# Two attention layers with output projection and layer norm, eight cores: how softmax sums are made and staged, how filler is dealt out, and what the output tiles wait for

## The chip, the cores and the metric

One Trainium2 chip; the program runs on all 8 cores, each on one of the 8 sequences of the batch, without exchange between cores. The metric is the device time in microseconds (us) of the slowest core, median of several runs. Engines are called PE (TensorE, matmul), DVE (VectorE), ACT (ScalarE), POOL (GpSimd) and SP (SyncE, here only a DMA queue).

## The reference

```python
def attn(x, Wqkv, bqkv, Wo, bo):            # 16 query heads of 128, ONE k and v head
    qkv = x @ Wqkv.T + bqkv                 # x: (8, 2048, 2048)
    s = q @ k.T / sqrt(128), causal;  p = softmax(s);  ctx = p @ v
    return ctx @ Wo.T + bo
def ffn(x, Wa, Wp, w_std, w_rec):           # 16 heads with q, k and v of their own
    fused = x @ (Wa * col_scale)            # 120 "std" + 8 "low" columns a head for q and k
    # low columns of q and k change places where w_rec > 0.1
    s = Qf @ Kf.T / sqrt(128), causal;  return concat(softmax(s) @ V) @ Wp
x = layernorm(x + attn(x));  x = layernorm(x + ffn(x))
```

A core does 2048 rows by 2048 columns in bf16 matmuls with f32 accumulation.

## The kernel before

**Program.** A Python builder (`Prog`) writes down each engine's instructions in order. Every operation gives a token (semaphore, count) and may wait for tokens of others. Within an engine the order is exactly the order in which the builder was called, so that where a line stands in the builder is where it stands in the queue. Loads that cast f32 to bf16 go through POOL's queue; all other transfers go through SP's queue.

**Stages.** (1) x transposed (`xT`, in `bufB`) and the weights of k, v and the first q are loaded and projected. (2) `at1`: attention of 16 heads with the q projections of later heads as filler for PE. (3) `outproj`: context (`bufA`) times `wo` (in `bufB`), plus residual and bias, layer norm; rows are stored and a transposed copy is put into `bufA`. (4) `at2`: attention of 16 heads with q, k and v projections as filler. (5) `outproj` again with `wp`.

**One head.** The transposed scores are made in 20 steps (`STEPS`): four windows w of 512 queries; in window w, 2w "full" steps (two key blocks of 128 by 512 queries), then step "a" (512 + 384 columns) and step "b" (256 + 128 columns) on the diagonal, whose corners POOL masks. `WIN_END` is (1, 5, 11, 19). A step g counts on over all heads. `scores(g)` fills one of two banks `s_ps`, ACT's exp writes `pt` (four buffers), `values(g)` adds v times pt into `c_ps`, and at the end of a window ACT copies `c_ps` to one of the `cf` buffers. The loop `run` issues in step g: scores(g+1); hooks; `todo` (below); filler from a stream of generators until a target count is reached (`feed`, one unit is one matmul of 512 columns, 0.5 for one of 256); values(g-1); `lsum`.

**Softmax sums.** DVE adds the pt tiles of a window to `acc` (1024 columns), then folds its halves to 512 (`sums`). `split_hi` (ACT) and `split_lo` (DVE) make bf16 hi and lo of it; `lsum` lets PE add over the partitions with a band of ones, each window into 32 rows of `l_ps` of its own. `recip` (DVE) inverts `l_ps` in `r4`; SP stores one row of each window to DRAM (`rr_d`) and `bcast` loads it back into all partitions (`rb`); `norm` (DVE) multiplies `cf` by `rb` into the context. `plan` says at which step of this or the next head each is issued. at1 has two rb and six cf buffers, at2 one rb and five cf. Parameter `lag` (1 in at1, 0 in at2, 1 in at2's last head) delays split and lsum by that many steps and puts the sums of the next tile behind lo in DVE's queue. Window 0 is summed in `acc[:, 512:1024]`; a new window may be added only when lo of the old one has read acc. Windows 0 to 2 of the last head go the same way into buffers of their own (`rb_last`), window 3 in `tail` by ones-matmuls on hi and lo to all partitions.

**Shift.** For each head `stats` (a small matmul and a DVE maximum) and `shift` (a small matmul and a DVE maximum, `mbias`) estimate the exponent's offset. Both use the bank of `pj0`/`pj1` that the next filler group will use, whose first matmul then waits for them. `insert(n, ...)` places them n units further down the stream. A filler group (16 matmuls, or 32 of half the size) is 16 units.

**Around the last head.** After the last projection the streams give idle units (42 in at1, 46 in at2), then `early_tiles`: 14 of the 16 head terms of two output tiles. Big weight loads (2048 KB, four for each projection) are issued on POOL at the steps given in `at_step`, the last two after the loop. `outproj` then does parts of six tiles (heads 0 to 14), `tail`, z loads (SP; POOL adds the bias), and the rest. A tile is 16 matmuls into one of eight banks; DVE adds it to z and frees the bank. z buffers lie over q, pt, acc and k of the attention.

## Time and profile before

| | |
|---|---|
| median of 3 runs | 2178.45 us (2171.26 to 2179.46) |
| the profiled execution's own time | 2177.09 us |
| its span, slowest core (6) | 2175.2 us |
| spans of the eight cores | 2150.7 to 2175.2 us |
| PE busy | 1988.3 us, 91% |
| DVE busy | 1178.8 us, 54% |
| ACT busy | 1011.5 us, 46% |
| POOL busy | 263.1 us, 12% |

The profile is one execution. Busy time of PE counts matmuls, whose ends are modelled; weight loads run beside them. The clock is the one granted to PE as a part of full speed. "Idle before" is what an engine waited before a group, with the engine that ended it. In DVE and PE rows the name left of the arrow is written, those on the right are read; L298 is the projections' matmul, L412 scores, L424 exp, L574 values, L812 output tiles, L691 early output tiles, L540 norm, L513 reciprocal, L80 any DMA.

### The profile page before, as it was taken

The page shows a single profiled execution, that of the slowest core. Times are in us where ns is not written, and L with a number is a line of the kernel's source. Part 1 is how long each engine was busy: PE and PEld are TensorE (multiplying, and loading weights), DVE is VectorE, ACT ScalarE, POOL GpSimd, SP SyncE. Part 2 cuts the span into 40 slices and gives each one's busy share as a digit, 9 for nine tenths or more (in the row PEclk, how much of TensorE's full clock was granted, in tenths as well). Part 3 has the DMA queues.
Part 4 walks back from the last instruction along what each step waited for, and adds up shares of the span by engine and source line. Part 5 has one row for each costly group of instructions (what it writes and reads, how often), then busy time and mean ns, then how long its engine had stood idle before and what let it go on. Part 6 is the DMA issues. An engine that isn't in the chain of part 4 may idle for free.

```text
span 2175.2 us, 30749 instructions; the slowest of 8 cores (2150.7 to 2175.2 us)
## 1 busy us (share of the span) xinstructions
PE 1988.3 (91%) x10400; PEld 1007.4 (46%) x10400; DVE 1178.8 (54%) x1931; ACT 1011.5 (46%) x1403; POOL 263.1 (12%) x354
## 2 busy tenths in 40 slices
PE   5999898989877999999999999999999999769997
PEld 2444343434333444464655646464554646324443
DVE  0167878788876365314554545555554555543433
ACT  0266776777763343315454453535454453532221
POOL 2011111111111344100010100100010000110000
PEclk9788999999998999999999999999999999889999
DMA  9521212121136798612122212212122110375751
GB/s 145 89 39 30 50 40 52 38 54 35 38 60 112 173 278 236 166 31 37 40 50 49 49 31 45 44 30 59 40 49 49 45 35 16 59 119 139 223 206 78
DMA packets 94981, 171.68 MB, mean 79 GB/s; under 512 B 38126, under 2 KB 62830, under 8 KB 85484
## 3 DMA queue, kind: packets, MB, share of 16 engines
q0 software_dynamic: 33216, 59.77, 17.6%
q1 hardware_dynamic: 61612, 109.94, 17.4%
q8 instruction: 87, 1.43, 0.3%
q14 instruction: 66, 0.54, 0.1%
HBM read 187.26 MB, written 33.81 MB: 102 GB/s over the span
## 4 chain that ended last, share of the span: by engine, by line
PE 80%; DMA 7%; issue 4%; DVE 4%; ACT 3%; POOL 2%; DVEq 0%; SPq 0%; ACTq 0%; POOLq 0%; another core or an unknown queue 0%
PE pj L298 29%; PE pj L1016 10%; PE c_ps L574 10%; PE s_ps L412 9%; PE s_ps L812 9%; PE pj L812 4%; PE c_ps L812 2%; PE l_ps L812 2%; DMA bufB<-xT 2%; ACT pt L424 1%; DMA rb<-rr_res 1%; PE l_ps L505 1%; PE l_ps L506 1%; DMA rl<-rr_res 1%; DMA bufB<-wo 1%
## 5 line engine op out<-in xcount | busy, mean ns | idle before, releaser
L424 ACT ACTIVATE pt<-s_ps,mbias 128x1024 bf16<-128x1024 f32 (+2 forms) x640 | 631.0, 988 | 577.5 <-PE s_ps L412 493.1
L298 PE MATMUL pj<-bufA,ws 128*128 128x512 bf16 x2048 | 485.2, 381 | 17.8 <-DVE mbias L394 16.1
L574 PE MATMUL c_ps<-pt,v 128*128 128x512 bf16 (+3 forms) x1280 | 350.3, 356 | 43.4 <-ACT cf L584 34.7
L298 PEld LDWEIGHTS pj<-bufA,ws 128*128 128x128 bf16 x2048 | 199.0, 98 | 250.5 <-issue 26.8
L468 DVE TENSOR_TENSOR acc<-acc,pt 128x1024 f32<-128x1024 f32 x192 | 235.5, 1226 | 129.2 <-ACT pt L424 120.4
L298 PE MATMUL pj<-bufB,ws 128*128 128x512 bf16 x1024 | 288.8, 396 | 1.2 <-DVE mhat L381 0.7
L432 POOL TENSOR_SCALAR_AFFINE_SELECT pt<-pt 128x256 bf16<-128x256 bf16 x256 | 139.5, 546 | 988.4 <-ACT pt L424 986.5
L1016 PE MATMUL pj<-wv,bufA 128*128 128x256 bf16 x2048 | 240.0, 273 | 14.2 <-DVE mbias L394 13.5
L1016 PEld LDWEIGHTS pj<-wv,bufA 128*128 128x128 bf16 x2048 | 199.2, 98 | 53.4 <-issue 16.6
L574 PEld LDWEIGHTS c_ps<-pt,v 128*128 128x128 bf16 x1280 | 122.9, 99 | 200.2 <-issue 99.8
L837 ACT ACTIVATE sqs<-z 128x512 f32<-128x512 f32 x128 | 80.6, 629 | 247.6 <-DVE z L832 235.2
L495 DVE TENSOR_TENSOR lo<-acc,hi 128x512 bf16<-128x512 f32 x128 | 88.4, 690 | 184.9 <-ACT hi L490 180.9
L412 PE MATMUL s_ps<-q,kT 128*128 128x512 bf16 (+3 forms) x640 | 176.3, 359 | 2.2 <-ACT pt L424 1.8
L412 PE MATMUL s_ps<-q,k 128*128 128x512 bf16 (+3 forms) x640 | 172.8, 352 | 0.1
L298 PEld LDWEIGHTS pj<-bufB,ws 128*128 128x128 bf16 x1024 | 101.0, 101 | 113.8 <-issue 40.6
L462 DVE TENSOR_TENSOR acc<-pt,pt 128x1024 f32<-128x1024 bf16 x96 | 116.7, 1216 | 32.6 <-ACT pt L424 27.3
L812 PE MATMUL s_ps<-bufB,bufA 128*128 128x512 bf16 x512 | 116.1, 387 | 7.5 <-DVE bufA L540 5.8
L812 PE MATMUL s_ps<-bufA,bufB 128*128 128x512 bf16 x512 | 116.8, 389 | 0.0
L471 DVE TENSOR_TENSOR acc<-acc,pt 128x512 f32<-128x512 f32 x96 | 67.7, 705 | 90.0 <-POOL pt L432 89.9
L513 DVE RECIPROCAL r<-l_ps 128x512 f32<-128x512 f32 (+1 forms) x32 | 107.2, 3351 | 0.1
L584 ACT COPY cf<-c_ps 128x512 f32<-128x512 f32 x127 | 74.2, 584 | 56.5 <-PE c_ps L574 56.3
L412 PEld LDWEIGHTS s_ps<-q,k 128*128 128x128 bf16 x640 | 62.7, 99 | 71.3 <-issue 5.9
(110 smaller groups left out, 1770.7 us busy)
## 6 DMA issues: line engine op xcount, KB each, us to landing
rb<-rr_res SPq DMA_DIRECT2D x120, 256.0 KB, 3.5
ws<-wqk POOLq DMA_DIRECT2D x32, 512.0 KB, 5.2
z<-x SPq DMA_DIRECT2D x16, 1024.0 KB, 6.5
x_res<-z SPq DMA_DIRECT2D x16, 1024.0 KB, 6.4
z<-x_res SPq DMA_DIRECT2D x16, 1024.0 KB, 6.5
out<-z SPq DMA_DIRECT2D x16, 1024.0 KB, 7.2
ws<-wq POOLq DMA_DIRECT2D x16, 512.0 KB, 6.1
bufB<-wo POOLq DMA_DIRECT2D x4, 2048.0 KB, 27.4
```

The costliest lines, as they stand in the source:

```text
L298: tok = P.pe(lambda t, c=c, b=b: t.matmul(pj[b][:, :], lhs(c), rhs(c), start=(c == 0), stop=(c == NCH - 1)), waits=wt, inc=(c == NCH - 1))
L412: last = t.matmul(sp[:, o:o + n], k[:, c * 128:(c + 1) * 128], q[:, w * 512 + q0:w * 512 + q0 + n], start=True, stop=True)
L424: self.exp_tok[g] = P.ac(lambda s: s.activation(pt[:, 0:n], sp[:, 0:n], AF.Exp, bias=mbias[h % 2][:, :]), waits=[self.s_tok[g], self.mb_ok ...
L432: ok = P.gp(lambda g_: g_.affine_select(out=blk, in_=blk, pattern=[[0, 2], [1, 128]], compare_op=ALU.is_ge, fill=0.0, base=0, channel_mult ...
L462: t = P.ve(lambda v: v.tensor_add(acc[:, :], p0[:, :], pt[:, :]), waits=[ok, self.p_ok[g - 1], self.hl_src_read])
L468: t = P.ve(lambda v: v.tensor_add(acc[:, :], acc[:, :], pt[:, :]), waits=[ok, self.acc_ok])
L495: self.lo_ok = P.ve(lambda v: v.tensor_sub(self.lo[:, :], src, self.hi[:, :]), waits=[self.hi_ok, self.fold_ok, self.hl_free])
L513: self.r_tok[h] = P.ve(lambda v: v.reciprocal(self.r4[0:n, :], l_ps[0:n, :]), waits=[self.l_tok[h], self.ro_tok.get(h - 1)])
L574: last = t.matmul(c_ps[:, q0:q0 + n], self.vbuf(h)[:, c * 128:(c + 1) * 128], pt[:, o:o + n], start=(beg and n_ == 0), stop=(end and n_ == 1))
L812: last = t.matmul(banks[b], ctx[:, h * S + j * 128:h * S + (j + 1) * 128], wbuf[:, (ew * H + h) * 512:(ew * H + h + 1) * 512], start=(h == ...
L837: state["sq"] = P.ac(lambda s: s.activation(sqs[:, :], zc, AF.Square, accum_out=cq[:, ew:ew + 1]), waits=[t, state["sq"]])
L1016: tok = P.pe(lambda t, tt=tt, c=c, s0=s0: t.matmul(pj[b][:, tt * 256:(tt + 1) * 256], bufA[:, s0:s0 + 128], wv2[:, c * 256:(c + 1) * 256], ...
```

## The change

- xT lies in `bufB` by windows: [w][c][512] instead of [c][w 512]. So the quarter of window 0 is free for the first quarter of `wo` as soon as the last q group of window 0 is done, and it is loaded there. wp's first quarter is loaded at the last k projection.
- `fold_out` (at1): the fold of acc goes to a buffer of its own (`f1`), window 0 is summed there; hi and lo are double; a third rb.
- Steps of split, lsum, recip, norm and bcast are given by lists; in at1 split is at (3, 7, 13, 21) instead of (2, 6, 12, 20), lsum at (8, 9, 15, 22) instead of (5, 8, 14, 21), recip at 3 instead of 2, bcast at (6, 7, 8, 12) instead of (4, 5, 9, 11), norm at (10, 12, 14, 16) instead of (9, 11, 14, 16). In at1 the next sums stand between hi and lo.
- at1's filler is uneven: weight 6.0 at steps 1, 3, 7 and 13, else 2.5, of 64 a head (before 3.2 each); its lead falls from 36 to 30 units over the heads.
- Last head of both: no sums on DVE. `last_sums` multiplies each pt by a 128x128 of ones into pj0 or pj1, straight to all partitions; a reciprocal of the bank, then the norm, at each window's end. `tail` is gone.
- One whole early tile (16 matmuls, in `l_ps`, the first bank in the new order of banks) instead of two of 14; idle units 60 and 56.
- Output tiles wait for the norms of their own window of 512 rows in heads 14 and 15; z loads wait for the end of the last head's values (at1's fourth for its last norm).
- at2: `shift` at 22 units instead of 13.5. Last two quarters of wo and wp are loaded at step 13 of the last head.

```diff
-    hi1 = row("hi1", 36864, 512, BF16)
-    lo1 = row("lo1", 37888, 512, BF16)
+    hi1 = [row("hi1_0", 36864, 512, BF16), row("hi1_1", 24576, 512, BF16)]
+    lo1 = [row("lo1_0", 37888, 512, BF16), row("lo1_1", 25600, 512, BF16)]
+    f1 = [row(f"f1_{i}", 26624 + 2048 * i, 512, F32) for i in range(2)]
...
+    rb1.append(row("rb1_2", 30720, 512, F32))
...
+            t = P.dma("gpsimd", f"xt{w}_{i}", xT3[:, w, i * n:(i + 1) * n, :],
...
+        def sources(self, w):
+            if self.fold_out:
+                return (self.fold[0][:, :], 0) if w == 0 else (self.fold[1][:, :], 1)
+            return (self.acc[:, 512:1024], 0) if w == 0 else (self.acc[:, 0:512], 1)
...
+            if h == H - 1:
+                return
...
-                if w > 0:
-                    t = P.ve(lambda v: v.tensor_add(acc[:, 0:512], acc[:, 0:512],
-                                                    acc[:, 512:1024]), waits=[t])
-                self.fold_ok = t
+                self.fold_ok[w] = P.ve(lambda v: v.tensor_add(src, acc[:, 0:512],
+                                                              acc[:, 512:1024]),
+                                       waits=[t] + ([self.src_read[1]] if self.fold_out else []))
...
+            rb = self.rb[n] if h < H - 1 else self.fold[w % 2]
...
+        def last_sums(self, g):
+            h, i = g // NST, g % NST
+            w, kind, chunk = STEPS[i]
+            pt = self.pt[g % 4]
+            pcs = pieces(w, kind, chunk)
+            beg, end = i == WIN_BEG[w], i == WIN_END[w]
+            b = (w + 1) % 2
             ones = strip[:, 96:97].broadcast_to([128, 128])
             def mm(t):
-                t.matmul(l_ps[:, :], ones, self.hi[:, :], start=True, stop=False)
-                return t.matmul(l_ps[:, :], ones, self.lo[:, :], start=False, stop=True)
-            t = P.pe(mm, waits=[self.hi_ok, self.lo_ok, self.r_tok[h]])
-            for i in range(NW - 1):
-                self.norm(h, i)
-            self.rb_ok[(h, w)] = P.ve(lambda v: v.reciprocal(self.r4[:, :], l_ps[:, :]),
-                                      waits=[t, self.ro_tok[h]])
-            self.norm(h, w)
+                last = None
+                for n_, (c, q0, o, n) in enumerate(pcs):
+                    last = t.matmul(pj[b][:, q0:q0 + n], ones, pt[:, o:o + n],
+                                    start=(beg and n_ == 0), stop=(end and n_ == 1))
+                return last
+            t = P.pe(mm, waits=[self.p_ok[g], tok_strip] + ([pj_free[b]] if beg else []))
+            if end:
+                rb = self.fold[w % 2]
+                self.rb_ok[(h, w)] = P.ve(
+                    lambda v: v.reciprocal(rb[:, :], pj[b][:, :]),
+                    waits=[t, self.norm_tok[(h, w - 2)] if w > 1 else None] + self.src_read)
+                pj_free[b] = self.rb_ok[(h, w)]
...
+            if h == H - 1:
+                self.last_sums(g)
             t = P.pe(mm, waits=[self.p_ok[g], self.v_ok[(h, chunk)], self.v_ok[(h, chunk + 1)]] +
...
+                if h == H - 1:
+                    self.norm(h, w)
...
+            for h in range(H - 1):
+                g0, g1 = h * NST, (h + 1) * NST
                 for w in range(NW):
-                    if last and w == NW - 1:
-                        continue
-                    put(g0 + WIN_END[w] + lag, "split", h, w)
-                    put(g0 + self.l_at[w] + (lag if w < NW - 1 else 0), "lsum", h, w)
-                if last:
-                    put(g0 + 14 + lag, "recip", h)
-                    for w in range(NW - 1):
-                        put(g0 + 14 + lag, "bcast", h, w)
-                else:
-                    g1 = g0 + NST
-                    norm_at = self.norm_at if h < H - 2 else self.norm_at_last
-                    bc_at = self.bc_at if h < H - 2 else self.bc_at_last
-                    put(g1 + self.r_at, "recip", h)
-                    for w in range(NW):
-                        put(g1 + norm_at[w], "norm", h, w)
-                    for w in range(NW):
-                        put(g1 + bc_at[w], "bcast", h, w)
+                    put(g0 + self.split_at[w], "split", h, w)
+                    put(g0 + self.l_at[w], "lsum", h, w)
+                    put(g1 + self.norm_at[w], "norm", h, w)
+                    put(g1 + self.bc_at[w], "bcast", h, w)
+                put(g1 + self.r_at, "recip", h)
...
-                lag = self.lag if h < H - 1 or i == 0 else self.lag_last
-                if lag == 0 and g + 1 < n:
+                if not self.fold_out and g + 1 < n:
                     self.sums(g + 1)
                 for what, hh, w in todo:
                     if what == "split":
                         self.split_hi(w)
+                if self.fold_out and g + 1 < n:
+                    self.sums(g + 1)
                 for what, hh, w in todo:
                     if what == "split":
                         self.split_lo(w)
-                if lag == 1 and g + 1 < n:
-                    self.sums(g + 1)
...
+    at1 = Att("a1", 0, lambda h: kT, lambda h: q1[h % 2], lambda h: v1, bufA, pt1, acc1, f1,
+              True, hi1, lo1, cf1, rb1, r41, (3, 7, 13, 21), (8, 9, 15, 22), 3,
+              (6, 7, 8, 12), (10, 12, 14, 16))
...
+    def early_tile(att, ctx, wbuf, w_tok):
+        for h in range(H):
+            def mm(t, h=h):
+                return t.matmul(l_ps[:, :], ctx[:, h * S:h * S + 128],
+                                wbuf[:, h * 512:(h + 1) * 512], start=(h == 0),
+                                stop=(h == H - 1))
+            att.tile = P.pe(mm, waits=[w_tok[0], att.norm_tok[(h, 0)], att.r_tok[H - 2]],
+                            inc=(h == H - 1))
+            yield 1.0
...
+            if w == 0 and h == H - 1:
+                wo_tok.append(load_big(bufB, wo_d, 0, [tok]))
...
+    fill = [6.0 if i in (1, 3, 7, 13) else 2.5 for i in range(NST)]
+    def lead1(h):
+        return 36.0 - 6.0 * min(h, H - 1) / (H - 1)
     def target1(h, i):
-        return 64.0 * h + LEAD1 + 64.0 * (i + 1) / NST
+        a, b = 64.0 * h + lead1(h), 64.0 * (h + 1) + lead1(h + 1)
+        return a + (b - a) * sum(fill[:i + 1]) / sum(fill)
...
-    at1.at_step[(H - 2) * NST + 11] = lambda tok: wo_tok.append(
-        load_big(bufB, wo_d, 0, [xt_end[0], tok]))
-    at1.at_step[(H - 1) * NST + 10] = lambda tok: wo_tok.append(
+    at1.at_step[(H - 2) * NST + 13] = lambda tok: wo_tok.append(
         load_big(bufB, wo_d, 1, [xt_end[0], tok]))
+    at1.at_step[(H - 1) * NST + 13] = lambda tok: wo_tok.extend(
+        load_big(bufB, wo_d, i, [xt_end[0], tok]) for i in (2, 3))
     at1.run(target1)
-    for i in (2, 3):
-        wo_tok.append(load_big(bufB, wo_d, i, [xt_end[0]]))
...
-            b = turn[0] % 8
+            b = (7, 1, 2, 3, 4, 5, 6, 0)[turn[0] % 8]
...
+        def normed(w):
+            return [att.norm_tok[(h, w)] for h in (H - 2, H - 1)]
...
-        last = [att.norm_tok[(H - 2, NW - 1)]]
-        fin = {}
-        heads(2, 2, 0, range(H - 1), last + [w_tok[0], bank_free[2]], False)
-        att.tail()
-        for jj in first_z:
-            load_z(jj, zfree + [att.norm_tok[(H - 1, NW - 2)]])
-            add_bias(jj)
-        bank_free[7] = att.rb_ok[(H - 1, NW - 1)]
-        heads(3, 3, 0, range(H - 1), [bank_free[3]], False)
-        for j in (0, 1):
-            heads(j, j, 0, [H - 2], [], False)
-        for j in (0, 1):
-            heads(4 + j, j, 1, range(H - 1), [w_tok[1], bank_free[4 + j]], False)
-        for n in range(6):
-            fin[n] = heads(n, n % 4, n // 4, [H - 1], [att.norm_tok[(H - 1, NW - 1)]], True)
-        for n in range(4):
-            evict(n, n, 0, fin[n])
-        for n in range(6):
-            next_bank()
-        evict(4, 0, 1, fin[4])
-        evict(5, 1, 1, fin[5])
-        for ew in (1, 2, 3):
-            for j in range(2 if ew == 1 else 0, 4):
+        for j in first_z:
+            load_z(j, zfree[j])
+            add_bias(j)
+        for ew in range(4):
+            for j in range(4):
                 b = next_bank()
-                t = heads(b, j, ew, range(H), [w_tok[ew], bank_free[b]], True)
+                t = att.tile
+                if ew + j > 0:
+                    t = heads(b, j, ew, range(H),
+                              [w_tok[ew], bank_free[b]] + normed(0), True)
...
-                t = heads(b, j, ew, range(H), [bank_free[b]], True)
+                t = heads(b, j, ew, range(H),
+                          [bank_free[b]] + normed(j // 4), True)
...
+                            [[at1.pv_done[H - 1]]] * 3 + [[at1.norm_tok[(H - 1, NW - 1)]]], tok_bo, finish1,
...
+              acc2, f2, False, hi2, lo2, cf2, rb2, r42, (1, 5, 11, 19), (4, 6, 12, 20), 1,
+              (3, 5, 7, 9), (5, 7, 9, 11))
...
+                    wp_tok.append(load_big(bufA, wp_d, 0, [tok]))
...
-            at2.insert(13.5, lambda h=h: at2.shift(h))
+            at2.insert(22.0, lambda h=h: at2.shift(h))
...
-        for u in idle(46):
+        for u in idle(56):
             yield u
-        for u in early_tiles(at2, bufB, bufA, wp_tok):
+        for u in early_tile(at2, bufB, bufA, wp_tok):
...
+    at2.at_step[(H - 1) * NST + 7] = lambda tok: wp_tok.append(
         load_big(bufA, wp_d, 1, [x2_end[0], tok]))
+    at2.at_step[(H - 1) * NST + 13] = lambda tok: wp_tok.extend(
+        load_big(bufA, wp_d, i, [x2_end[0], tok]) for i in (2, 3))
```

## Rows read from the trace of the kernel before

**Rows 1.** The cores: span and mean granted clock, slowest core.

```profile
core 6: 2175.2 us, clock 0.964
```

**Rows 2.** Windows of core 6: length, busy us (instructions) of each engine, clock, DMA share, GB/s.

```profile
core 6: us, PE busy (x) PEld busy (x) DVE busy (x) ACT busy (x) POOL busy (x), PEclk, DMA share, GB/s
95.00:205.00 110.00, 106.71 (x434) 45.50 (x433) 75.30 (x101) 73.55 (x92) 14.02 (x25) 0.81 0.18 34
205.00:624.40 419.40, 372.91 (x1810) 170.25 (x1809) 337.88 (x456) 298.99 (x374) 60.99 (x103) 1.00 0.18 41
624.40:733.00 108.60, 77.57 (x317) 31.48 (x316) 58.45 (x77) 37.82 (x51) 32.10 (x23) 0.86 0.77 138
...
980.00:1870.00 890.00, 861.38 (x5016) 487.96 (x5015) 472.47 (x736) 425.19 (x529) 74.61 (x149) 0.99 0.19 41
1875.50:1962.50 87.00, 55.39 (x209) 21.77 (x208) 44.09 (x53) 28.27 (x35) 10.33 (x14) 0.79 0.73 114
1962.50:2163.00 200.50, 200.50 (x929) 90.76 (x927) 76.65 (x231) 49.86 (x142) 0.00 (x0) 1.00 0.50 165
```

**Rows 3.** Waits of PE, 160 to 590: us in total, times, longest.

```profile
PE c_ps L574 <- ACT cf L584: 24.8, 43, 1.1
PE l_ps L505 <- DVE r L513: 18.1, 12, 1.9
```

**Rows 4.** DVE's groups by form, 160 to 590: busy, mean ns; idle before, releaser.

```profile
L513 DVE RECIPROCAL r<-l_ps 128x512 f32<-128x512 f32 x12 | 40.2, 3352 | 0.0
L495 DVE TENSOR_TENSOR lo<-acc,hi 128x512 bf16<-128x512 f32 x48 | 33.1, 690 | 51.9 <-ACT hi L490 47.8 <-ACT cf L584 4.0
```

**Rows 5.** Waits of PE, 980 to 1870.

```profile
PE pj L298 <- DVE mbias L394: 16.1, 7, 2.3
PE pj L1016 <- DVE mbias L394: 12.6, 7, 1.8
```

**Rows 6.** Waits of PE, 0 to 95.

```profile
PE pj L298 <- DMA bufB<-xT: 26.1, 7, 13.7
```

**Rows 7.** PE in order of time, 590 to 740: start, us, what; idle before, releaser.

```profile
650.38 0.59 PE L691 MATMUL pj<-bufB,bufA 128*128 128x512 bf16 x1 [7.51 <-DMA bufB<-wo]
...
687.27 6.19 PE L812 MATMUL s_ps<-bufB,bufA 128*128 128x512 bf16 x15 [5.80 <-DVE bufA L540]
...
708.10 1.01 PE L812 MATMUL pj<-bufB,bufA 128*128 128x512 bf16 x2 [4.06 <-DVE bufA L540]
```

**Rows 8.** POOL in order of time, 600 to 735.

```profile
680.95 2.32 POOL L80 DMA_DIRECT2D bufB<-wo  x2
...
714.05 17.92 POOL L825 TENSOR_TENSOR z<-z,bo_sb 128x2048 f32<-128x2048 f32 x4 [29.16 <-DMA z<-x]
```

**Rows 9.** The chain that ended last, in order of time: start, us, what.

```profile
1880.33 17.35 DMA bufA<-wp
1909.18 2.97 DMA rb<-rr_res
1913.01 6.49 DMA rb<-rr_res
1920.35 8.46 DMA rb<-rr_res
...
1936.79 5.19 DMA rr_res<-r
```

**Rows 10.** PE in order of time, 1850 to 1980.

```profile
1885.66 0.58 PE L505 MATMUL l_ps<-hi,strip 128*128 128x512 bf16 x1 [3.25 <-DVE lo L495]
...
1897.82 1.44 PE L691 MATMUL pj<-bufA,bufB 128*128 128x512 bf16 x3 [7.63 <-DMA bufA<-wp]
...
1932.52 0.91 PE L574 MATMUL c_ps<-pt,v 128*128 128x512 bf16 x2 [4.60 <-POOL pt L432]
...
1959.96 1.01 PE L812 MATMUL pj<-bufA,bufB 128*128 128x512 bf16 x2 [5.29 <-DVE bufB L540]
```

**Rows 11.** DVE in order of time, 1860 to 1980.

```profile
1886.85 3.36 DVE L513 RECIPROCAL r<-l_ps 128x512 f32<-128x512 f32 x1
```

More of the change, by code:

```diff
@@ L220, in build_program @@
     acc2 = row("acc2", 36864, 1024, F32)
-    hi2 = row("hi2", 40960, 512, BF16)
-    lo2 = row("lo2", 41984, 512, BF16)
+    hi2 = [row("hi2", 40960, 512, BF16)]
+    lo2 = [row("lo2", 41984, 512, BF16)]
+    f2 = [row(f"f2_{i}", 38912 - 2048 * i, 512, F32) for i in range(2)]
     cf2 = [row(f"cf2_{i}", 43008 + 2048 * i, 512, F32) for i in range(5)]
@@ L684, in idle @@
             yield 1.0
-    def early_tiles(att, ctx, wbuf, w_tok):
-        for j in (0, 1):
-            for h in range(H - 2):
-                wt = [w_tok[0], att.norm_tok[(h, NW - 1)], pj_free[j]]
-                P.pe(lambda t, j=j, h=h: t.matmul(
-                    banks[j], ctx[:, h * S + j * 128:h * S + (j + 1) * 128],
-                    wbuf[:, h * 512:(h + 1) * 512], start=(h == 0), stop=False),
-                    waits=wt, inc=False)
-                yield 1.0
+    def early_tile(att, ctx, wbuf, w_tok):
[7 more added lines that the diff above has]
+            yield 1.0
     def q1_group(h, w):
```

158 lines of the change are left out of this document (63 added, 95 removed).

## The prediction, made before the changed kernel ran

> **What bounds the kernel now.** I read the cores first: the slowest is core 6, at 2175.2 us [rows 1]; the execution's own time is 2177.09 us, so 1.9 us lie around the span. The windows of core 6 [rows 2] cut it into stages. TensorE (PE) does nearly all of the path: the second output projection runs at 100% busy and clock 1.00, 929 matmuls in 200.5 us, 0.2158 us each. So a gain can come only where PE is idle or at a lower clock. That is: 46.5 us in the first attention at full clock (205 to 624.4), 28.6 us in the second (980 to 1870), 31.0 us at the first change-over (clock 0.86), 31.6 us at the second (clock 0.79). From 95 to 205 the clock is 0.81 and PE idles only 3.3 us.
>
> What PE waits for in the first attention [rows 3]: in 430 us, 43 times for ScalarE's (ACT's) copy cf out of c_ps (24.8 us), 12 times for VectorE's (DVE's) reciprocal (18.1 us). The rows by form of DVE [rows 4] show one reciprocal of 3.35 us a head, 12 in 430 us: a head takes 35.8 us. They also show DVE idle 47.8 us before the 48 subtractions lo, waiting for ACT's hi: 4.0 us a head.
>
> In the second attention [rows 5] every wait of PE is for mbias, the shift, 14 times, 28.7 us.
>
> **Change, start of the program.** xT lies in blocks of w instead of c. PE waits 26.1 us for xT [rows 6], 13.7 of it for the first piece. The same bytes come in the same ten transfers, so at best the later 12 us shrink (half of it if larger pieces help), at worst nothing: 0 to -6, I take -0.5.
>
> **First attention, per head.** No operation is added or taken; order, buffers and waits change. (a) hi, lo move one step later: cf is now ahead of hi in ACT's queue, where hi waits for the fold. (b) lo stands behind the next sums, so DVE works where it waited 4.0 us. (c) `lsum` of window 0, which must wait for the reciprocal of the head before, is issued at step 8 and the reciprocal at 3: PE's wait for it (18.1/12 = 1.5 us a head) has five steps of cover, against three. (d) Filler: 6 units at steps 1, 3, 7, 13, just where `values` waits for cf, instead of 3.2. That puts 2.8 x 0.2158 = 0.6 us more work ahead of a wait whose mean is 24.8/43 = 0.58 us. The other steps get 0.7 units (0.15 us) less. So both PE waits should go. The floor is now double. PE: 372.91/419.4 x 35.8 = 31.8 us a head. DVE: 337.88/419.4 x 35.8 = 28.8 busy; of its idle 6.9, the 4.0 for hi can go and the rest are hand-overs: 31.8 as well. Two engines with equal floors, coupled by four pt buffers, and cf(2) that waits (on ACT) for the norm of the head before, which stands behind a late DVE: they don't both reach it. I take 32.6 us, so 3.2 x 11.7 heads = -37. Bounds: -46 (all idle), -12 (DVE late, 1 us a head). In the stretch at clock 0.81 PE is nearly full: 0 to -3.3, I take -2.
>
> **First change-over.** Before: projections end at 624.4, the projection's matmuls at 916, 291.6 us. After: head 14 has 11 steps left without filler. PE needs some 8 us for them, but DVE still sums them. Before, PE stood at the early tiles at 642.9 (650.38 less 7.51 [rows 7]), 18.5 us later and two steps further; I take 16. Head 15: scores, values and now ones-matmuls, each 17408 columns = 34 x 0.2158 = 7.3 us, together 22.0; the early tile 16 x 0.2158 = 3.5; the last band sums 0.4: 26, of which 1.5 overlap the tail before. DVE loses all sums of that head and gets four reciprocals (3.35 each) for two. Stalls 3 us: the last lo, and the norm of head 14, behind two reciprocals in a row (15's first, then 14's), which the tile's 15th matmul wants at step 13. Then 63 tiles x 3.453 = 217.5, for which only the norms of window 0 are needed, long done. Sum 16 + 24.5 + 3 + 217.5 = 261: -30. What goes by name: 7.51 (wo), 5.80 and 4.06 (the norms) [rows 7]. What may come late next: z is loaded from the end of head 15 and POOL adds the bias in 17.92/4 = 4.5 us each [rows 8]; as before about 10 us until z is there, then four adds, 14 to 28 us. PE needs its first bank again after seven tiles, 24 us, and that bank waits only for z0. Covered by 10 us. The two big loads in front of the last two masks on POOL cost 2.32 us of issue [rows 8], under five steps of about 1.3 us: nothing; without that cover 2.3. Bounds: -37 and -20.
>
> **Second attention.** `shift` goes from 13.5 to 22 units behind its head's last projection. A group is 16 units; before, the shift used the bank that the group starting 2.5 units later needs, and PE waited 28.7/14 = 2.05 us for DVE. Now the bank's next group begins ten units (2.2 us) and about one attention step later: 2.05 + 0.54 = 2.6 us of latency under some 3 us. mbias itself is needed 14 units later at the earliest. So -29; at least -5, if DVE's queue is late by more than one sum of 1.2 us.
>
> **Second change-over.** Before: from 1875.5 to 2163.1, 287.6 us. wp starts with the last projection, 5 us earlier, and lands at about 1875.7 + 17.35 + 0.8 = 1894 [rows 9]; PE, which stood at step 3 at 1890.2 (1897.82 less 7.63 [rows 10]), comes to the tile three steps and 4 us later, also about 1894: the 7.63 goes. Of the other idle the 3.25 for lo stays, the 4.60 for a mask (behind DVE's late sums) and the 5.29 for the norms go [rows 10]. Of head 15's 26 us some 6 are done at 1894; with 4 us of stalls (ACT's copy of window 1 waits for head 14's first norm) PE would be through at about 1918. But at2 has one rb buffer, so head 14's four broadcasts go one by one, each after the norm before. And the second tile now goes to bank 1, which is pj1, free only after the reciprocal of window 2, which stands on DVE behind the last of those norms. Chain: reciprocal 1886.85 + 3.36 [rows 11]; store 5.19 to 1895.4; first broadcast 3 to 6.5, norm and hand-over 0.9 (1913.01 less 1909.18 + 2.97), 1900.5; three more beside the wp loads at 6.49 to 8.46 [rows 9] plus 0.9, 25.2; 1926; reciprocal 3.35, 1929.5; 2 us for a PE that restarts at half clock (1.2 GHz, as in the 15 matmuls in 6.19 us [rows 7]). 1931.5 + 217.5 = 2149: -14. Ends: all broadcasts as quick as the free one (2.97 [rows 9]) makes PE the limit, -27; 12 us each gives +3.
>
> The DMA share of this chain is where a rule bears. The rows show a broadcast at 2.97 us alone and 8.46 beside the loads [rows 9]. The Trainium skill (DMA: Bandwidth & Descriptors, section Queues, rings and completion order) says each DMA engine takes turns between queue rows: two more loads in POOL's queue would then not slow SP's broadcasts further, and the sum stands. If they shared by transfer, four at once would make 4 x 2.97 = 12 us, two broadcasts later by 4 each, 8 us worse. Only before and after together can tell.
>
> **Sum.** -0.5 - 2 - 37 - 30 - 29 - 14 = -112.5. On the execution's own 2177.09: 2064.6; the median of the runs, 2178.45, lies 1.4 above: 2066.
>
> **Rivals.** (1) DVE becomes the bound of the first attention: its floor equals PE's [rows 2, 4]; for it, a queue with a 3.35 us reciprocal in one lump; against it, four pt buffers. A head of 34.8 us: 25 lost, 2091. (2) The shift's wait moves instead of going, at the other bank, behind DVE's copies of v: 24 lost, 2090. (3) "Tiles wait for their own block" isn't so where banks bind: the chain through bank 1 is longer (12 us broadcasts), or the same one binds in at1 too: 15 lost, 2081. Against it in at1: three rb buffers, and window 2's reciprocal stands before the last two norms. (4) Slower: PE denser on all cores draws the clock of 0.81 over the attention. Its price: PE's 861 us in the second attention alone become 861/0.81, +202; it decides once some 480 us more of full PE run at 0.81 (112/0.235), 2066 + 202 = 2268 for that stage. For it: 95 to 205 [rows 2]. Against it: 200.5 us at 100% busy and clock 1.00. The Trainium skill (TensorE: Matmul & The Clock Gate, Part 1) has a limiter that holds a die at 13/16 once three of its cores run dense matmuls; the row of the output projection speaks against it here.
>
> **Chances.** Forecast 0.65; (1) 0.13, (2) 0.08, (3) 0.10, (4) 0.04. Range: all good ends together 2029, all bad 2144; neither is likely, 2046 (PE near its floor in both) to 2104 (rivals 1 to 3, or two of them in part) leaves out 0.2. Its own range for the forecast is 2046 to 2085. Half a per cent, about what a measurement of this kernel can tell from no change, is 11 us; only the last rival and a heap of misses reach it: faster 0.94, same 0.02, slower 0.04.
>
> **What will show it.** Right: one reciprocal each 32 to 33 us in the first attention, no waits for cf or r at `values` and `lsum`, DVE over 90% there; no PE wait for mbias in the second; no gap over 2 us between head 15 and the tiles in at1; in at2 a PE gap before the second tile that DVE's reciprocal ends, at about 1929 less what went before. Wrong: ACT waiting for DVE's sums or norms in each head, a granted clock under 1.00 for long, or tiles waiting for z.

## The result, and the profile after

The changed kernel takes 2054.37 us (median of four executions, three of which lie between 2052.94 and 2055.14), 0.9443 of before's time (95% interval 0.9418 to 0.9468): 5.6% faster. I had forecast 2066, with a range of 2046 to 2104. Of both kernels some executions are longer, with four cores at a lower clock (here one of 2308.19 us, at 0.85 to 0.87), and all ratios, and the times given further down, leave these out.

The profiled execution took 2052.94 us. Its cores, with mean granted clock:

```profile
core 0: 2041.3 us, clock 0.991
...
core 7: 2051.1 us, clock 0.989
```

Before, the slowest core had a clock of 0.964 [rows 1]; now none is under 0.988. The windows of core 7, at the landmarks used in the prediction (last projection at 567.5 and 1767, last matmul of the two output projections at 835.3 and 2038.9):

```profile
core 7: us, PE busy (x) PEld busy (x) DVE busy (x) ACT busy (x) POOL busy (x), PEclk, DMA share, GB/s
95.00:205.00 110.00, 105.26 (x521) 49.41 (x519) 90.28 (x121) 85.82 (x109) 17.49 (x30) 1.00 0.16 35
205.00:567.50 362.50, 342.12 (x1694) 162.02 (x1693) 318.27 (x428) 276.99 (x350) 63.21 (x97) 1.00 0.23 52
567.50:617.50 50.00, 41.62 (x194) 18.28 (x192) 37.55 (x38) 34.38 (x40) 10.98 (x16) 0.93 0.57 99
617.50:835.30 217.80, 217.76 (x1011) 98.56 (x1008) 98.56 (x237) 77.45 (x158) 73.95 (x20) 1.00 0.88 214
980.00:1767.00 787.00, 783.00 (x4656) 452.28 (x4655) 436.26 (x679) 382.56 (x476) 67.20 (x135) 1.00 0.20 43
1767.00:1819.10 52.10, 33.86 (x160) 15.30 (x158) 23.71 (x20) 25.90 (x31) 9.34 (x14) 0.84 0.89 147
1819.10:2038.90 219.80, 219.76 (x1008) 99.01 (x1008) 81.71 (x234) 49.83 (x142) 0.00 (x0) 0.99 0.52 157
```

From these landmarks, slowest core against slowest core, and core 0 against core 0 (in us). The last projection of the first attention ends at 623.7 in before, not at 624.4 where the prediction cut its windows:

| up to / between | before, core 6 | after, core 7 | difference | core 0 | predicted |
|---|---|---|---|---|---|
| start to last projection of attention 1 | 623.7 | 567.5 | -56.2 | -43.9 | -39.5 |
| to the end of output projection 1 | 292.4 | 267.8 | -24.6 | -20.0 | -30 |
| to the last projection of attention 2 | 959.4 | 931.7 | -27.7 | -32.5 | -29 |
| to the end of output projection 2 | 287.6 | 271.9 | -15.7 | -13.1 | -14 |
| sum | | | -124.2 | -109.5 | -112.5 |

Core 0's first attention ran at clock 1.00 in both kernels, while cores 6 and 7 of before had 0.81 from 95 to 205 [rows 2]. It is one of six such cores, and the six don't agree closely: their sums go from -107.9 to -126.0, with a mean of -115.0. The means of the four stages are -44.6, -23.9, -30.4 and -16.1.

The waits of PE (us in total, times, longest) from 160 to 560 of after:

```profile
PE l_ps L523 <- DVE lo L512: 19.4, 25, 1.2
PE pj L394 <- ACT q L702: 2.4, 4, 0.7
PE pj L301 <- DVE mhat L384: 0.8, 1, 0.8
```

The waits for ACT's cf and for DVE's reciprocal, 24.8 and 18.1 us in 430 us [rows 3], are gone. In their place stands a wait at the same matmul (L505 is now L523) for lo. DVE over the same stretch waits for the masks, and no longer for hi: the second fence, its groups by form, has no idle ahead of the 49 subtractions lo, against 51.9 us [rows 4]. DVE is busy for 350 of these 400 us, 87.5%:

```profile
DVE acc L487 <- POOL pt L435: 27.9, 33, 1.8
```

```profile
L512 DVE TENSOR_TENSOR lo<-f,hi 128x512 bf16<-128x512 f32 x49 | 36.0, 735 | 0.0
```

From 980 to 1767, where PE lost 28.7 us to mbias [rows 5], it waits only for this:

```profile
PE pj L394 <- DVE v L1016: 4.0, 7, 0.6
```

The first change-over, PE in order of time. The tiles start without a gap; the gaps for wo and for the norms [rows 7] are gone:

```profile
597.30 0.38 PE L690 MATMUL l_ps<-bufB,bufA 128*128 128x512 bf16 x1 [2.35 <-DVE r L530]
...
617.37 0.33 PE L588 MATMUL c_ps<-pt,v 128*128 128x256 bf16 x2
617.53 3.62 PE L817 MATMUL pj<-bufB,bufA 128*128 128x512 bf16 x16
```

The second, PE and then DVE. Of the waits for wp and for a mask [rows 10] only 0.23 us are left, but the second tile stands 11.44 us:

```profile
1776.99 0.59 PE L523 MATMUL l_ps<-hi,strip 128*128 128x512 bf16 x1 [3.96 <-ACT cf L601]
...
1807.21 0.33 PE L567 MATMUL pj<-pt,strip 128*128 128x256 bf16 x2 [0.23 <-POOL pt L435]
1819.14 5.67 PE L817 MATMUL pj<-bufA,bufB 128*128 128x512 bf16 x16 [11.44 <-DVE f L574]
```

```profile
1776.15 0.69 DVE L512 TENSOR_TENSOR lo<-acc,hi 128x512 bf16<-128x512 f32 x1 [1.78 <-ACT hi L506]
1778.17 3.36 DVE L530 RECIPROCAL r<-l_ps 128x512 f32<-128x512 f32 x1 [1.33 <-PE l_ps L524]
...
1788.14 0.69 DVE L545 TENSOR_TENSOR bufB<-cf,rb 128x512 bf16<-128x512 f32 x1 [2.23 <-DMA rb<-rr_res]
...
1796.81 0.69 DVE L545 TENSOR_TENSOR bufB<-cf,rb 128x512 bf16<-128x512 f32 x1 [3.84 <-DMA rb<-rr_res]
1806.10 0.69 DVE L545 TENSOR_TENSOR bufB<-cf,rb 128x512 bf16<-128x512 f32 x1 [8.60 <-DMA rb<-rr_res]
1815.03 0.69 DVE L545 TENSOR_TENSOR bufB<-cf,rb 128x512 bf16<-128x512 f32 x1 [8.23 <-DMA rb<-rr_res]
1815.64 3.35 DVE L574 RECIPROCAL f<-pj 128x512 f32<-128x512 f32 x1
```

This is the chain: the reciprocal of head 14, four norms (L545) each waiting for its broadcast, and only then the reciprocal of window 2 (L574) that frees bank 1 for the second tile.

### The profile page after: what moved, and what is told of

Its sections match the earlier page's. It is cut to its first block, busy times and chain, and to the rows that moved or that the text cites. A ratio compares the mean times of both kernels' runs of the same rounds, so it can differ in the third digit from the quotient of the medians.

```text
span 2051.1 us, 30678 instructions; the slowest of 8 cores (2037.6 to 2051.1 us)
## 1 busy us (share of the span) xinstructions
PE 1946.3 (95%) x10464; PEld 1006.8 (49%) x10464; DVE 1146.5 (56%) x1871; ACT 1001.6 (49%) x1395; POOL 261.5 (13%) x354
## 4 chain that ended last, share of the span: by engine, by line
PE 73%; DVE 10%; issue 5%; ACT 5%; DMA 4%; POOL 2%; DVEq 0%; another core or an unknown queue 0%; ACTq 0%; POOLq 0%; SPq 0%
PE pj L301 24%; PE s_ps L817 11%; PE pj L1007 10%; PE s_ps L415 7%; PE c_ps L588 7%; PE pj L817 5%; ACT pt L427 4%; PE c_ps L817 3%; DVE r L530 3%; PE l_ps L817 2%; DMA bufB<-xT 2%; DMA rb<-rr_res 2%; POOL pt L435 1%; DVE acc L489 1%; PE l_ps L523 1%
## 5 line engine op out<-in xcount | busy, mean ns | idle before, releaser
L588 PE MATMUL c_ps<-pt,v 128*128 128x512 bf16 (+3 forms) x1280 | 341.9, 349 | 4.0 <-ACT cf L601 3.7
L484 DVE TENSOR_TENSOR acc<-acc,pt 128x1024 f32<-128x1024 f32 x180 | 220.5, 1225 | 126.9 <-ACT pt L427 123.8
L301 PE MATMUL pj<-bufB,ws 128*128 128x512 bf16 x1024 | 272.6, 379 | 2.0 <-DVE mhat L384 1.5
L415 PE MATMUL s_ps<-q,kT 128*128 128x512 bf16 (+3 forms) x640 | 170.6, 349 | 2.1 <-ACT pt L427 2.1
L478 DVE TENSOR_TENSOR acc<-pt,pt 128x1024 f32<-128x1024 bf16 x90 | 109.3, 1215 | 36.6 <-ACT pt L427 33.7
L817 PE MATMUL s_ps<-bufA,bufB 128*128 128x512 bf16 x512 | 111.8, 379 | 0.0
L512 DVE TENSOR_TENSOR lo<-acc,hi 128x512 bf16<-128x512 f32 x60 | 42.9, 715 | 111.3 <-ACT hi L506 108.4
L840 DVE SCALAR_TENSOR_TENSOR z<-s_ps,z 128x512 f32<-128x512 f32 x64 | 43.5, 689 | 105.0 <-PE s_ps L817 94.7
L530 DVE RECIPROCAL r<-l_ps 128x512 f32<-128x512 f32 x30 | 100.4, 3348 | 1.3 <-PE l_ps L524 1.3
```

Of the source, the lines that this page charges most:

```text
L301: tok = P.pe(lambda t, c=c, b=b: t.matmul(pj[b][:, :], lhs(c), rhs(c), start=(c == 0), stop=(c == NCH - 1)), waits=wt, inc=(c == NCH - 1))
L415: last = t.matmul(sp[:, o:o + n], k[:, c * 128:(c + 1) * 128], q[:, w * 512 + q0:w * 512 + q0 + n], start=True, stop=True)
L478: t = P.ve(lambda v: v.tensor_add(acc[:, :], p0[:, :], pt[:, :]), waits=[ok, self.p_ok[g - 1], self.fold_ok[w - 1] if w > 1 else self.fold ...
L484: t = P.ve(lambda v: v.tensor_add(acc[:, :], acc[:, :], pt[:, :]), waits=[ok, self.acc_ok])
L530: self.r_tok[h] = P.ve(lambda v: v.reciprocal(self.r4[:, :], l_ps[:, :]), waits=[self.l_tok[h], self.ro_tok.get(h - 1)])
L588: last = t.matmul(c_ps[:, q0:q0 + n], self.vbuf(h)[:, c * 128:(c + 1) * 128], pt[:, o:o + n], start=(beg and n_ == 0), stop=(end and n_ == 1))
```

## Experiments

Ratios are to before. The changed kernel run again (e0_after) shows how far two runs of one kernel differ: 0.9463 (0.9447 to 0.9478), median 2056.97; so 0.002 can be noise. In its profile the gap ahead of the second tile was 15.14 us.

> The kernel after, unchanged, as the reference for the three beside it. A head of its first attention takes 33.0 us; all its windows should be as in its first profile, within 3 us in total.

**The shift alone**, in the kernel before.

```diff
-            at2.insert(13.5, lambda h=h: at2.shift(h))
+            at2.insert(22.0, lambda h=h: at2.shift(h))
```

> The kernel before with one edit: the second attention's shift stands 22 units behind the last projection of its head instead of 13.5. My theory (the wait for mbias disappears under the next filler group) expects the 28.7 us of waits in the second attention to go and nothing else to change: 29 us less than before, ratio 0.987. The rival (the wait moves to the other bank, behind the copies of v) expects 5 us less at most, ratio 0.998.

0.9846 (0.9831 to 0.9862), 2138.83 us against 2171.85: -33. From 980 to 1830 all waits for mbias went; one of another kind is left:

```profile
PE pj L391 <- DVE v L1025: 4.0, 7, 0.6
```

The span from output projection 1 to the last projection is 931.0 us here and 931.7 in after. So this edit makes the whole gain of that stage, and the wait did not move to the other bank. It gives 4 us more than the waits held. The trace of before shows where they lie. Its core 0 waits for mbias no longer than core 6 (28.5 us), but in five places the clock granted to PE falls while or just after it waits (0.83 to 0.92 over the 10 us from 1004, 1124, 1244, 1494 and 1614), and its stage takes 964.4 us; core 6 has three such places and 959.4. In after no stretch of 10 us from 980 to 1767 is under 1.00, nor in this run to 1832. So in some places a wait of 2.3 us cost its own length and some 3 us at half clock after it (core 0, 1130 to 1132: clock 0.50).

**The old schedule of attention 1 in the changed kernel**: buffers and both change-overs of after; the order of sums and lo, steps and filler of before (the lead of the filler stays that of after).

```diff
-    fill = [6.0 if i in (1, 3, 7, 13) else 2.5 for i in range(NST)]
+    fill = [3.2 for i in range(NST)]
...
-(3, 7, 13, 21), (8, 9, 15, 22), 3, (6, 7, 8, 12), (10, 12, 14, 16)
+(2, 6, 12, 20), (5, 8, 14, 21), 2, (4, 5, 9, 11), (9, 11, 14, 16)
```

> The kernel after with the schedule of the kernel before in the first attention: even filler, split at 2, 6, 12, 20, lsum at 5, 8, 14, 21, reciprocal at 2, broadcasts and norms at the old steps, lo ahead of the next sums. What stays of the change there is room alone: folds in buffers of their own, hi and lo double, a third rb. Theory A (the order made the gain, each part of it sharing it with the others): a head goes back to 35 us or more, 28 to 38 us slower than after. Rival B (room made the gain: the next window's sums need not wait for lo): a head stays under 34 us, less than 14 us slower. Lo first alone cost 3 to 4 us and even filler alone 9, so their sum, 13, is what B would expect at most.

2088.94 and 2090.55 us; two executions, too few for a ratio: +32 to +36. The reciprocals give the head's length: 14 of them from 134.5 to 593.1 are 35.3 us a head. PE's waits from 160 to 560 are those of before again:

```profile
PE c_ps L588 <- ACT cf L601: 24.0, 46, 0.9
PE l_ps L523 <- DVE r L530: 15.3, 11, 1.5
```

With 36.0 a head in before (below) and 33.0 in after, the order is worth 2.3 us a head and the rest, the doubled and separate buffers among it, some 0.7.

**Only the splits back to the old steps**, a step earlier.

```diff
-(3, 7, 13, 21), (8, 9, 15, 22), 3,
+(2, 6, 12, 20), (8, 9, 15, 22), 3,
```

> The kernel after with only the splits back at steps 2, 6, 12, 20 in the first attention, so that ACT's hi stands ahead of the copy cf again. If hi ahead of cf, waiting for the fold, was what kept PE waiting at the window ends, a head grows by 1 to 2 us, 14 to 28 us slower than after. If the filler of 6 units covers it as well, or VectorE is the bound anyway: within 5 us of after.

0.9597 (0.9583 to 0.9611), median 2087.59: +29 to +33. Reciprocals 133.8 to 590.5 (14): 35.1 a head. From 160 to 560, PE's wait and then ACT's:

```profile
PE c_ps L588 <- ACT cf L601: 33.8, 23, 2.6
```

```profile
ACT hi L506 <- DVE f L499: 35.9, 23, 2.6
```

The same count, the same longest wait: ACT stands at hi for the fold, cf stands behind it, and PE waits for cf. Step (a) taken back alone takes back nearly all that the old schedule does (2.1 of 2.3 us a head).

It does so by other waits than those of before. Here PE waits 23 times, 1.5 us on average; in before 43 times, 0.58 [rows 3], and with the whole old schedule 46 times, 0.52. There ACT hardly waits for the fold: 8.3 us in the 430 of before, 0.5 at most, and 5.3 in the 400 of the old schedule. What the copy cf waits for in before is mostly hi itself, which stands ahead of it in ACT's queue, as ACT's rows show for the wait of 0.51 that PE has at 596.74:

```profile
595.50 0.61 ACT L490 CAST hi<-acc 128x512 bf16<-128x512 f32 x1
596.00 0.59 ACT L584 COPY cf<-c_ps 128x512 f32<-128x512 f32 x1
```

In between lie the place of lo, the filler and the later steps, which this run keeps from after; which of them makes the long waits isn't shown. So this run shows that the new order needs (a); whether (a) alone would have brought the gain to the kernel before, no run shows.

**lo ahead of the next sums again**: the two blocks of `run` exchanged for attention 1.

```diff
-                if self.fold_out and g + 1 < n:
-                    self.sums(g + 1)
                 for what, hh, w in todo:
                     if what == "split":
                         self.split_lo(w)
+                if self.fold_out and g + 1 < n:
+                    self.sums(g + 1)
```

> The kernel after with lo put ahead of the next tile's sums again in VectorE's queue, in the first attention only. Theory (VectorE is the second floor of a head there, 33.0 us measured, and the new order saved it 4.0 us a head of waiting for hi): the head grows by 1 to 3 us, 14 to 40 us slower than after, the waits of lo for hi come back. Rival (the gain of the first attention came from the filler and from lsum's later step alone): under 5 us slower.

0.9461 (0.9444 to 0.9478): no difference that can be told, where I expected 14 to 40 us. The head stays 33.0 (129.2 to 591.1, 15 reciprocals). DVE stands 26.9 us ahead of lo again (the trace puts 7.9 to hi and 19.0 to PE's scores), and PE waits 9.2 for lo instead of 19.4, but also for mhat and cf:

```profile
PE l_ps L523 <- DVE lo L512: 9.2, 13, 1.0
PE pj L301 <- DVE mhat L384: 4.4, 6, 1.3
PE c_ps L588 <- ACT cf L601: 4.1, 6, 1.2
```

Step (b) only exchanges one wait for others.

**Even filler**, `fill = [3.2 for i in range(NST)]`.

> The kernel after with even filler in the first attention, 3.2 units at every step instead of 6.0 at four and 2.5 at sixteen. Theory: the waits of PE for the copy cf come back, four of about 0.6 us a head, but part of them only takes the place of waits for VectorE, which is as full as PE: 10 to 30 us slower than after. Rival (uneven filler does nothing, since hi no longer stands ahead of cf): within 5 us.

0.9486 (0.9471 to 0.9501), all four executions between 2059.88 and 2060.88: +5 to +9 us. Reciprocals 131.0 to 600.6 (15): 33.5 a head, half a microsecond more. But the waits for cf don't come back:

```profile
PE l_ps L523 <- DVE lo L512: 23.7, 24, 2.0
PE c_ps L588 <- ACT cf L601: 1.5, 1, 1.5
```

So step (d) is worth about what I gave it (0.6 us), not for the reason that I gave: the filler's 6 units don't cover cf, since with (a) nothing waits for cf anyway.

**DVE made lighter**: in attention 1 every plain "full" sum adds only the first 512 of its 1024 columns, so the row sums are incomplete.

```diff
             elif kind == "full":
-                t = P.ve(lambda v: v.tensor_add(acc[:, :], acc[:, :], pt[:, :]),
+                c = 512 if self.fold_out else 1024
+                t = P.ve(lambda v: v.tensor_add(acc[:, 0:c], acc[:, 0:c], pt[:, 0:c]),
```

> The kernel after, with half of the columns left out of the plain additions of full tiles (the 1024-column additions after a window's first) in the first attention: VectorE has some 3 us less to do in a head, PE exactly the same. If VectorE's floor binds a head (31.8 us by my estimate, against 31.8 for PE), the head falls from 33.0 to 31.5 or less, 20 us or more faster than after. If PE's own work and its small waits make the 33.0: under 8 us faster. In between: both floors bind in turn, which is my theory: 8 to 20 us faster.

0.9392 (0.9373 to 0.9410): -11 to -15 us; reciprocals 134.0 to 579.8 (15), 31.8 a head. PE's first wait from 160 to 560, and the window (PE, PEld, DVE, ACT, POOL):

```profile
PE l_ps L524 <- DVE lo L513: 9.0, 21, 1.1
```

```profile
160.00:560.00 400.00, 389.03 (x1926) 184.18 (x1924) 323.11 (x484) 315.99 (x400) 56.33 (x110) 1.00 0.24 53
```

A head falls by 1.2 us and stops at PE's floor of 31.8 [rows 2], with PE at 97%. DVE thus costs attention 1 the 1.2 us between the floor and 33.0. That PE pays it at `lsum` suggests a cheaper way to give it back:

**`lsum` and reciprocal later.**

```diff
-(3, 7, 13, 21), (8, 9, 15, 22), 3,
+(3, 7, 13, 21), (8, 10, 15, 23), 4,
```

> The kernel after with lsum at steps 8, 10, 15, 23 instead of 8, 9, 15, 22 and the reciprocal at 4 instead of 3, in the first attention: the two lsum of a head that PE waits for (27 waits for lo, 20.4 us in 450) come one step later. If PE's small waits add straight to the time: 15 to 20 us faster than after. If VectorE, which is busy nearly without a break, is the bound of a head, the time stays within 5 us. The lighter VectorE of the run before gave 15 us, so I expect something between: 5 to 12 us faster.

0.9425 (0.9400 to 0.9449); against after -4 to -8 us, at the edge of what can be told by its time. The trace is plainer: reciprocals 134.6 to 582.4 (15), 32.0 a head, and the wait for lo is gone:

```profile
PE pj L301 <- DVE mhat L384: 7.2, 5, 2.3
PE c_ps L588 <- ACT cf L601: 3.2, 4, 1.5
...
PE l_ps L523 <- DVE lo L512: 0.7, 1, 0.7
```

No work was taken from DVE. So what bound the head at 33.0 was not DVE's amount of work but that PE asked for lo too early.

**Bank 1 last in the turn.** The tiles of both output projections take their banks in another order.

```diff
-            b = (7, 1, 2, 3, 4, 5, 6, 0)[turn[0] % 8]
+            b = (7, 2, 3, 4, 5, 6, 1, 0)[turn[0] % 8]
```

> The kernel after with the output tiles' banks in the order 7, 2, 3, 4, 5, 6, 1, 0, so that the bank of window 2's reciprocal (1) is wanted by the seventh tile instead of the second. Theory: the 11.4 us in which PE waits for that reciprocal at the second change-over goes, with the half clock behind it: 11 to 14 us less than after. Rival (the broadcasts, the weights or z hold the next tiles just as long): under 3 us less.

0.9429 (0.9414 to 0.9444): -3 to -7, not the 11 to 14 expected. The tiles follow head 15 with no gap, 13 us earlier than in after, and PE stops later, for the third quarter of wp:

```profile
1805.88 13.98 PE L817 MATMUL s_ps<-bufA,bufB 128*128 128x512 bf16 x63
...
1838.38 1.86 PE L817 MATMUL l_ps<-bufA,bufB 128*128 128x512 bf16 x4 [8.16 <-DMA bufA<-wp]
```

That settles the place of the chain: only the order of the banks was changed, and the 11.4 us went. Most of them came back at the next thing in line.

**wp later**: the second quarter at step 14 of head 15 instead of 7, the others after it, banks as in after.

```diff
-    at2.at_step[(H - 1) * NST + 7] = lambda tok: wp_tok.append(
+    at2.at_step[(H - 1) * NST + 14] = lambda tok: wp_tok.append(
         load_big(bufA, wp_d, 1, [x2_end[0], tok]))
-    at2.at_step[(H - 1) * NST + 13] = lambda tok: wp_tok.extend(
-        load_big(bufA, wp_d, i, [x2_end[0], tok]) for i in (2, 3))
     at2.run(target2)
+    for i in (2, 3):
+        wp_tok.append(load_big(bufA, wp_d, i, [x2_end[0]]))
```

> The kernel after with wp's second quarter loaded at step 14 of the second attention's last head instead of 7, and its last two behind the loop instead of at step 13. The second to fourth broadcast of head 14 then have the DMA engines to themselves. Theory (the chain of four broadcasts, made slow by the weight loads, sets the moment at which the second tile gets its bank): the three broadcasts take 3 to 4 us each instead of about 8, the gap before the second tile shrinks from 11 to 15 us to 2 or less; what is saved can be lost again to wp's later quarters, so the time is 0 to 8 us below after. Rival (the broadcasts are slow whatever else moves): gap unchanged, and the later loads make it 5 us slower or more.

0.9454 (0.9435 to 0.9473): no gain. Left alone, the broadcasts cost DVE 3.4 and 3.5 us, and then PE stands for wp:

```profile
1797.19 0.69 DVE L545 TENSOR_TENSOR bufB<-cf,rb 128x512 bf16<-128x512 f32 x1 [3.41 <-DMA rb<-rr_res]
1801.39 0.69 DVE L545 TENSOR_TENSOR bufB<-cf,rb 128x512 bf16<-128x512 f32 x1 [3.50 <-DMA rb<-rr_res]
...
1833.36 8.87 PE L817 MATMUL s_ps<-bufA,bufB 128*128 128x512 bf16 x31 [15.14 <-DMA bufA<-wp]
```

**Bank order, and wp earlier** (quarters at steps 1, 6 and 11).

> The kernel after with the banks in the order 7, 2, 3, 4, 5, 6, 1, 0 and wp's later quarters issued at steps 1, 6 and 11 of the last head instead of 7, 13 and 13. With the bank order alone the gap before the second tile had gone, but PE waited 8.2 us for wp's third quarter. Theory: with the loads back to back from the first one on, that wait goes too: 12 to 18 us faster than after, ratio to before about 0.939. Rival (the DMA engines can't bring four quarters and z sooner than about 60 us after the first issue, whatever the order): the wait only moves, to z or the last quarter: within 3 us of the bank order alone.

0.9432 (0.9414 to 0.9451): the same as the bank order alone, and not the 12 to 18 us expected. The wait for wp is gone, and the first broadcasts of head 14, now beside the loads, come late: DVE's norm holds ACT's cf, and PE waits for it inside head 15:

```profile
1798.36 0.69 DVE L545 TENSOR_TENSOR bufB<-cf,rb 128x512 bf16<-128x512 f32 x1 [10.13 <-DMA rb<-rr_res]
```

```profile
1799.87 1.01 PE L588 MATMUL c_ps<-pt,v 128*128 128x512 bf16 x2 [7.98 <-ACT cf L601]
```

**The best together**: bank order, later `lsum` and reciprocal, and wp's quarters at steps 7, 10 and 13.

> The changed kernel with three edits together: the later band sums and reciprocal of e5_lsum_later (worth 4 to 8 us there), the bank order of e4_bank_order (3 to 6 us there, where a wait of 8.2 us for the third quarter of wp took back part of the gap of 11.4), and the load of that quarter three steps earlier, at step 10 instead of 13, the last one staying at 13. Theory (the two gains lie in different stages and add up; the earlier load takes the 8.2 away and slows a broadcast that nothing waits for any more): 8 to 15 us under the changed kernel, 2040 to 2047, ratio near 0.938, no PE wait over 3 us for wp or for DVE's reciprocal between head 15 and the tiles. Rival (the broadcasts and the loads share one path, so time taken off one is put on the other, as in e10_wp_later and e11_bank_loads): the wp wait goes but ACT's copy of c_ps waits for a norm, some 6 to 8 us, and the sum is that of e5_lsum_later alone, ratio 0.941 to 0.943.

0.9337 (0.9283 to 0.9391), executions from 2032.75 to 2049.14 with a median of 2033.74: some 20 us under after, more than the 8 to 15 expected. After was not run beside it, and before was slower there than elsewhere (median 2183.34), so this ratio can't be set against the others; the times can. In the profiled execution of 2037.84 us, the last projection of attention 1 stands at 558.3 (-9.2) and the second change-over with its output projection takes 266.8 (-5.1). What PE still waits for from 1745 to 1850:

```profile
PE l_ps L817 <- DMA bufA<-wp: 5.5, 1, 5.5
PE l_ps L523 <- ACT cf L601: 4.0, 1, 4.0
PE c_ps L588 <- ACT cf L601: 3.5, 2, 2.5
PE pj L394 <- DVE mhat L384: 1.0, 1, 1.0
```

The two gains lie in different stages and add up. The wait for wp did not fall under 3 us, as the theory wanted, but to 5.5. The profile accounts for 15 of the 20 us; why the median lies 4 us under the profiled execution isn't shown.

## Why the prediction was right

The total was partly luck. On the six cores whose clock was the same in both kernels the first attention gave 5 us more than I said and the first change-over 6 less (means of -44.6 and -23.9 against -39.5 and -30); the misses cancel.

**First attention, -37 on 11.7 heads.** Right in size, a little off in each factor. Reciprocals on core 0, before and after:

```profile
L513 DVE RECIPROCAL r<-l_ps x15: 3349/3351/3352, 133.1 to 637.3; 128x512 f32<-128x512 f32 x15
```

```profile
L530 DVE RECIPROCAL r<-l_ps x15: 3343/3345/3349, 129.4 to 590.2; 128x512 f32<-128x512 f32 x15
```

504.2 us became 460.8 over 14 heads: 36.0 to 32.9, where I took 35.8 to 32.6. Core 0's -43.9 up to the last projection is these 14 heads; I counted 11.7 because core 6 spent the first of them at clock 0.81, and gave that stretch 2. Of the four edits, (a) is the one without which the gain is lost (2.1 us, shown by the early splits), though not for the reason given: in before hi waited for the fold only 8.3 us in 430, and what cf lost was mostly hi's own 0.6 us ahead of it. (b), which I credited with DVE's 4.0 us of idle, can be taken back at no loss (shown by lo first). (d) gives 0.5. (c) wasn't tried alone. "Both PE waits should go": they did; what I did not name is the wait for lo that took part of their place (19.4 us). Its step is in (b) and (c): lo was moved back behind the next sums while `lsum` of windows 1 to 3 follows only one or two steps after its split. DVE's row did not fill over 90% either, as I had said it would, but to 87.5%: most of the idle that it no longer spends on hi it now spends on the masks (27.9 us).

**Rival 1, DVE as the bound** (34.8 us a head) fell: the head is 33.0, and with the same work on DVE it came to 32.0. That DVE costs something as soon as it's late was right: 1.2 us a head.

**The clock.** I gave the stretch at 0.81 a gain of 0 to 3.3 us with the clock as it was. Instead it was absent: the granted clock from 95 to 205 is 1.00 in after, and on core 0 of before too. In the profile of before it belongs to two cores; the next comparison's before, with no core under 0.975, had a median of 2171.85. It is no single event, though: of the nine executions of before beside the last experiment, six have two to four cores at a mean clock of 0.962 to 0.969, and take 2180.22 to 2195.41 us, against 2170.62 to 2173.61 for the three without. Of the 124.2 us between the two profiles' slowest cores some 5 to 10 are therefore not the change's: the slowest core of before without that stretch took 2169.8 us, 118.7 more than the slowest of after, and the mean of six is 115.0. This is an argument from those cores; no run set the clock, and whether the change made the stretch rarer isn't shown. Rival 4 fell as well. PE is busy 99% of the second attention at clock 1.00, denser than before, and so is every other core of its die (777 to 783 of 787 us).
**First change-over, -30.** Measured -24.6 (core 0: -20.0), inside the bounds of -37 and -20. The tiles take 217.8 as said (217.5). Mis-sized is "stalls 3 us": the 50.0 us up to the tiles were to be 43.5, PE waits about 8 in them (the largest 2.35 for the reciprocal and 2.12 for cf), and the window's clock is 0.93. z was covered, and so were the mask and the big loads.

**Second attention, -29.** -27.7 on the slowest core, -32.5 on core 0, and -33 from the edit alone. Rival 2 fell.

**Second change-over, -14.** Measured -15.7 (core 0: -13.1). The chain named in the prediction is the one in the trace, down to its last link: the gap ends with DVE's reciprocal of window 2 and PE restarts at half clock (granted 0.50 until 1822.7; 16 matmuls in 5.67 us, where they take 3.62 at the first change-over). It was shown by the bank order. The time fits as well: I had put the end of the gap at 1929 less what went before, which is 108.5 by core 7's last projection, so at 1820.5; it ended at 1819.0. PE's wait of 3.96 us at head 14's last `lsum` is the one for lo that I let stand. The row names ACT's cf, but `lsum` waits for hi and lo only, and lo ends at 1776.84, 0.15 us before PE starts. Behind it stands another link: lo waits 1.78 for hi, and hi stands on ACT behind an exp that waited 3.37 us for DVE's mbias. Nothing in the change shortens that.

**The DMA share in it.** In after the second broadcast took 7.81 us from issue to landing, beside one load of wp, the third and fourth 8.43 and 8.07 beside up to three (DVE's waits of 8.60 and 8.23); in e0_after the same three took 9.29, 9.49 and 9.23; before, one beside the loads took 8.46 [rows 9]; with the loads out of the way 3.1 to 3.3. By the Trainium skill's rule (DMA: Bandwidth & Descriptors, section Queues, rings and completion order) more loads in POOL's queue should not slow SP's broadcasts further, and the traces agree: one load or three made no difference of more than 0.6 us, and the 12 us of a share by transfer did not occur. What the rule doesn't say, and the experiments show, is that time given to one of the two is taken from the other: later loads bring a wait of 15.1 for wp, earlier ones a wait of 8.0 for a norm.

**Start, -0.5.** PE waited 27.6 us for xT, the longest 14.5, against 26.1 and 13.7 [rows 6]: the layout gave nothing.

## What to carry to other kernels

When an engine waits for a copy, look at what stands ahead of that copy in its engine's queue: without moving one cast a step later some 30 us of the gain here are lost, and without moving the work that it "frees" nothing is. A wait that ends at an engine with a nearly full row is not proof that the engine is the bound; ask for its result a step later before making it lighter. At a change of stage follow each PSUM bank back to its last reader: here the tile waited for the bank, not for its data, and the order in which banks are taken is free to change. Then ask what comes next in line: of the 11.4 us that the bank gave, 8.2 went to a load.

## What the hardware showed unexpectedly

Two kernels whose profiles differ by 124 us on their slowest cores differ by 107.9 to 126.0 on the six cores that ran at clock 1.00 from 95 to 205 in both: a clock of 0.81 held two of eight cores of before for 110 us, and the cores of one execution are 13 to 19 us apart even without that. Waits of 2.3 us were followed in some places, on some cores, by a few matmuls at half clock, so that removing 28.5 us of waits gave core 0 a stage 33 us shorter. And a broadcast of one row to 128 partitions, 256 KB, took 3.1 to 3.3 us on a free queue and 7.8 to 9.5 beside 2 MB loads of another queue, so that from the first of the four norms to the last it is 13.0 us with wp later and 28.6 with wp earlier.
